# A decoder layer on one core: batch 0's front as its own order on each engine, adapters staged elsewhere

## The reference

```python
# attention, 16 heads of 32
q, k, v = heads(x @ Wq + bq), heads(x @ Wk + bk), heads(x @ Wv + bv)
scores = normalised(q) @ normalised(k).T / (sigmoid(x.mean(axis=1) @ Wt + bt) + 0.5)
vals, idx = top_k(scores, S // 4)            # keep the 64 largest of each row of 256
attn = softmax(vals) scattered to idx
gate = sigmoid(x @ Wg + bg)
x = layernorm(x + gate * ((attn @ v) @ Wo + bo) + (1 - gate) * x)
# cross attention with the context as key and value
s = (x @ xWq + xbq) @ (ctx @ xWk + xbk).T
x = layernorm(x + softmax(s) @ (ctx @ xWv + xbv))
# adapters: 8 of 32 matrices of 512 by 512, chosen by ids, summed with weights
x = layernorm(x + x @ sum_k(w[k] * W[ids[k]]).T + sum_k(w[k] * b[ids[k]]))
```

## Time and profile before

| | us |
|---|---|
| median of 3 runs (3546.75 to 3565.47) | 3558.0 |
| the profiled execution | 3552.69 |
| its span | 3550.8 |
| PE busy | 2939.5 (83%) |
| DVE busy | 2754.0 (78%) |
| ACT busy | 2140.6 (60%) |
| POOL busy | 1797.6 (51%) |

### The profile page before, as it was taken

One profiled execution on the slowest core, in us unless ns is written; L12 is line 12 of the kernel. 1 busy time (PEld: TensorE's weight loads), 2 busy tenths in 40 slices (PEclk: granted clock), 3 DMA queues, 4 the chain that ended last, 5 costly groups with the idle time before them and its releaser, 6 DMA issues. The chain is left out here.

```text
span 3550.8 us, 59586 instructions
## 1 busy us (share of the span) xinstructions
PE 2939.5 (83%) x16154; PEld 1615.6 (45%) x16154; DVE 2754.0 (78%) x9472; ACT 2140.6 (60%) x5970; POOL 1797.6 (51%) x2285
## 2 busy tenths in 40 slices
PE   6798988878898689797887889788988889879755
PEld 3344444444454345454444445444544444444433
DVE  3787877878787787887878778787878888778872
ACT  2666666656666456665655667566665666566541
POOL 4355545545544455454554455465544556446533
PEclk9899999989998899999999999999989999899977
DMA  5000000000000000000000000000000000000000
GB/s 204 7 16 22 22 23 19 23 4 23 22 22 19 4 22 22 22 20 4 23 22 22 20 22 5 22 23 22 22 20 5 23 22 23 22 19 16 4 16 12
DMA packets 43575, 80.46 MB, mean 23 GB/s; under 512 B 3786, under 2 KB 11978, under 8 KB 43058
## 3 DMA queue, kind: packets, MB, share of 16 engines
q1 hardware_dynamic: 41554, 69.18, 5.8%
q0 software_dynamic: 1504, 5.77, 0.5%
HBM read 58.16 MB, written 16.78 MB: 21 GB/s over the span
## 5 line engine op out<-in xcount | busy, mean ns | idle before, releaser
L517 POOL TENSOR_SCALAR probs<-probs,kept_inv 128x256 f32<-128x256 f32 x1024 | 528.7, 536 | 892.1 <-DVE kept_inv L1769 892.1
L1730 DVE SCALAR_TENSOR_TENSOR probs<-scores,threshold,probs 128x256 f32<-128x256 f32 x1006 | 432.4, 493 | 206.9 <-issue 134.7
L1029 PE MATMUL work_ps<-ident,probs 128*128 128x128 f32 x2072 | 333.0, 297 | 182.9 <-POOL probs L517 123.6
L807 ACT ACTIVATE probsT<-work_ps 128x512 f32<-128x512 f32 x512 | 294.4, 596 | 303.8 <-PE work_ps L1029 287.9
L772 ACT ACTIVATE scores<-score_ps,neg_guess 128x256 f32<-128x256 f32 x1024 | 397.1, 483 | 103.7 <-DVE kept_inv L1769 98.1
L792 ACT ACTIVATE near<-scores 128x256 f32<-128x256 f32 x1024 | 412.8, 421 | 24.3 <-DVE nearest L1698 22.5
L1694 DVE MATCH_REPLACE8 near<-nearest,near 128x256 f32<-128x256 f32 x1024 | 406.9, 407 | 0.0
L1690 DVE MAX8 nearest<-near 128x8 f32<-128x256 f32 x1024 | 358.3, 411 | 6.3 <-DVE near L1682 4.7
L1029 PEld LDWEIGHTS work_ps<-ident,probs 128*128 128x128 f32 x2072 | 241.6, 149 | 263.2 <-POOL probs L517 120.2
L1698 DVE MAX8 nearest<-near 128x8 f32<-128x256 f32 x1024 | 356.9, 409 | 0.0
L484 POOL TENSOR_TENSOR inv_norm<-sumsq,minus_half 128x32 f32<-128x32 f32 x64 | 351.3, 5490 | 5.3
(11 more groups left out here) (171 smaller groups left out, 5535.4 us busy)
## 6 DMA issues: line engine op xcount, KB each, us to landing
x_in<-in_x_dram SPq DMA_DIRECT2D x32, 512.0 KB, 3.9
x_res<-in_x_dram SPq DMA_DIRECT2D x32, 512.0 KB, 4.6
out_dram<-rows SPq DMA_DIRECT2D x32, 512.0 KB, 3.1
c_sb<-in_ctx_dram SPq DMA_DIRECT2D x32, 256.0 KB, 2.7
scores<-in_L_ffn_W_dram SPq DMA_DIRECT2D x6, 1024.0 KB, 6.8
near<-in_L_ffn_W_dram SPq DMA_DIRECT2D x2, 1024.0 KB, 10.0
w_q<-in_L_attn_Wq_dram POOLq DMA_DIRECT2D x1, 1024.0 KB, 8.1
w_k<-in_L_attn_Wk_dram POOLq DMA_DIRECT2D x1, 1024.0 KB, 10.0
```

The lines of the kernel that those rows point to most:

```text
L517: pool.tensor_scalar(probs[:, s % 2, h, j], probs[:, s % 2, h, j], kept_inv[:, s % 2, n:n + 1], 1.0, ALU.mult, ALU.mult).then_inc(s_pr, 1)
L807: act.activation(probsT[:, h, 2 * a:2 * a + 2], W[BANK_TP[s][2 * h + a]][:].rearrange("p (h k n) -> p h k n", h=2, k=NT), ACT.Copy).then_i ...
L1029: last = pe.transpose(dst[:, n * P:n * P + P], part, ident[:])
L1730: step.mark(dve.scalar_tensor_tensor(out=probs[:, r, h, j], in0=scores[:, r, h, j], scalar=threshold[:, r, k:k + 1], in1=probs[:, r, h, j] ...
```

## The change

The front of batch 0 is no longer written by the passes "fill" and "first" (each step in them has got a condition `where != "fill"` or `where != "first"`), but as a list of its own ahead of `body(-1, ...)` on each engine. `fuse()` is gone; its parts are steps of these lists. PE's list in full, since the others answer to it:

```diff
             setup()
+            turn_x(0, 0)
+            turn_x(0, 1)
+            key(0, 0)
+            pe.wait_ge(s_xt, 2)
+            temp(0)
+            query(0, 0)
+            pe.wait_ge(s_qc, 1)
+            query(0, 1)
+            pe.wait_ge(s_tmp, 1)
+            key(0, 1)
+            pe.wait_ge(s_xt, 1)
+            turn_raw(1, 0).then_inc(s_fill, 1)
...
+            turn_raw_key(6, 1).then_inc(s_fill, 1)
+            pe.wait_ge(s_empty, 3)
+            cross_weights(7, 0).then_inc(s_fill, 1)
+            pe.wait_ge(s_empty, 6)
+            turn_query(0, 0)
+            pe.wait_ge(s_empty, 4)
+            turn_key(0, 0)
...
+            cross_weights(9, 2).then_inc(s_fill, 1)
+            pe.wait_ge(s_q16, 1)
+            pe.wait_ge(s_qt, 1)
+            adapter_bias(10).then_inc(s_fill, 1)
+            pe.wait_ge(s_kt, 1)
+            turn_query(0, 1)
+            pe.wait_ge(s_empty, 10)
+            turn_key(0, 1)
...
+            key_sums(0)
+            pe.wait_ge(s_empty, 9)
+            key_moments(0)
+            pe.wait_ge(s_empty, 8)
+            cross_weights(11, 3).then_inc(s_fill, 1)
+            pe.wait_ge(s_kt, 2)
+            cross_bias(12).then_inc(s_fill, 1)
+            pe.wait_ge(s_m, 1)
+            row_means(0)
+            pe.wait_ge(s_mu, 1)
+            row_moments(0, 0)
+            pe.wait_ge(s_empty, 12)
+            row_moments(0, 1)
+            make_scores(0, 0, 0)
+            pe.wait_ge(s_qu, 1)
+            gate(0, 0)
+            pe.wait_ge(s_empty, 11)
+            gate(0, 1)
+            pe.wait_ge(s_kf, 1)
+            turn_adapters(13, 0).then_inc(s_fill, 1)
...
+            turn_adapters(16, 3).then_inc(s_fill, 1)
+            late_weights()
             body(-1, 1, "fill")
             body(0, 0, "first")
```

The parts of `fuse()` may now use all four banks (`FILL_BANK`), one bank per step. The adapters are staged in buffers that batch 1 uses first, in two halves each, and DVE adds them by halves:

```diff
-        f_stage = [scores[:, 0].rearrange("p a h k -> p (a h k)"), scores[:, 1].rearrange("p a h k -> p (a h k)"),
-                   near[:].rearrange("p a h k -> p (a h k)")]
+        f_stage = [[rows[:, 4], rows[:, 5]],
+                   [gate_t[:, 1].rearrange("p t d -> p (t d)"), v_sb[:, 1].rearrange("p t d -> p (t d)")],
+                   [kT[:, 1].rearrange("p g k -> p (g k)"), rows[:, 6]]]
```

The loads on SP are issued in another order. The ids come first, wt_cols and neg_bt have a semaphore of their own (`s_temp`), bq_cols is the last of the short vectors, the raw weights stand ahead of the id loads, and x of batch 1 stands ahead of adapter 5:

```diff
+                    sp.dma_start(ids_sb[:], fids.rearrange("(a k) -> a k", a=1)).then_inc(s_ids, 16)
+                    load_x(0)
+                    for b, (g, a) in ((abk, BK), (abq, BQ), (abg, BG), (abv, BV)):
...
+                    sp.dma_start(bq_cols[:], xbq.rearrange("(a p) -> p a", p=P)).then_inc(s_late, 16)
+                sp.wait_ge(s_wk, 16)
+                sp.dma_start(raw_wq, xWq.rearrange("(a p) n -> p a n", p=P)).then_inc(s_rawx, 16)
+                sp.dma_start(raw_wk, xWk.rearrange("(a p) n -> p a n", p=P)).then_inc(s_rawx, 16)
                 sp.wait_ge(s_ids, 16)
...
                 for k, n in enumerate(ids):
                     if k >= 3:
-                        sp.wait_ge(s_fused, k - 2)
+                        sp.wait_ge(s_fused, 2 * (k - 2))
+                    if k == 5:
+                        load_x(1)
```

DVE waits in `setup()` only for the four biases, and widens wt_cols after the split. ACT waits for neg_bt after it has taken the first key. In a product of batch 0 only the last matmul waits for the split biases:

```diff
-            def project(dst, src, w, bias, t, kts=KD):
+            def project(dst, src, w, bias, t, kts=KD, first=False):
                 for kt in range(kts):
                     pe.matmul(dst, src[:, kt, t * P:t * P + P], w[:, kt], start=kt == 0, stop=False)
+                if first:
+                    pe.wait_ge(s_bias, 1)
                 return add_bias(dst, bias)
```

DVE's list, in full:

```diff
             setup()
+            split_biases(0)
+            widen_temp()
+            key_sums(0, 0)
+            temperature(0)
+            query_sums(0, 0)
+            query_sums(0, 1)
+            adapters(0, 1)
+            key_sums(0, 1)
+            adapters(1, 2)
+            adapter_shares()
+            adapters(2, 3)
+            split_late_biases()
+            adapters(3, 4)
+            query_moments(0, 0)
+            query_moments(0, 1)
+            moments(0)
+            after_guesses()
+            adapters(4, 5)
+            adapters(5, 6)
+            adapters(6, 7)
+            adapters(7, 8)
```

More of the change, by code:

```diff
@@ L421, in _ @@
             load_ctx(0)
-            load_x(1)
             load_x(2)
@@ L570, in body @@
                 if ahead:
-                    norms(i + 1, 0)
+                    if where != "fill":
+                        norms(i + 1, 0)
                 if behind:
@@ L581, in body @@
                 if ahead:
-                    norms(i + 1, 1)
+                    if where != "fill":
+                        norms(i + 1, 1)
                 if behind:
@@ L593, in body @@
                 if ahead:
-                    guesses(i + 1)
+                    if where != "fill":
+                        guesses(i + 1)
                 if here:
@@ L603, in _ @@
             setup()
+            norms(0, 0)
+            normalise(0, 0)
+            norms(0, 1)
+            normalise(0, 1)
+            guesses(0)
             body(-1, 1, "fill")
@@ L909, in body @@
                 if here:
-                    if where == "first":
-                        fuse()
-                    exps(i, 0, 0)
+                    if where != "first":
+                        exps(i, 0, 0)
                 if behind:
@@ L915, in body @@
                 if here:
-                    exps(i, 0, 1)
+                    if where != "first":
+                        exps(i, 0, 1)
                 if behind:
@@ new lines, in turn_raw, with turn_raw_key, cross_weights @@
+            def turn_raw(n, et):
+                if n == 1:
+                    pe.wait_ge(s_rawx, 32)
+                return turn(W[FILL_BANK[n]], [raw_wq[:, dt, et * P:et * P + P] for dt in range(KD)])
+            def turn_raw_key(n, e2):
+                return turn(W[FILL_BANK[n]], [raw_wk[:, ct, et * P:et * P + P] for et in (2 * e2, 2 * e2 + 1)
+                                              for ct in range(KC)])
+            def cross_weights(n, dt):
+                pe.wait_ge(s_empty, TURNED)
+                for et in range(KD):
+                    mm = pe.matmul(W[FILL_BANK[n]][:, 0:C], wqT[:, et, dt * P:dt * P + P], wkT[:, et],
+                                   start=et == 0, stop=et == KD - 1)
+                return mm
@@ L1093, in fuse @@
-                pe.wait_ge(s_fused, NW)
-                pe.wait_ge(s_empty, n)
-                for dt in range(KD):
-                    n += 1
-                    if dt >= 2:
-                        pe.wait_ge(s_empty, n - 2)
-                    turn(T[n % 2], [f_sum[:, ot * D + dt * P:ot * D + dt * P + P] for ot in range(KD)])\
-                        .then_inc(s_fill, 1)
-                pe.wait_ge(s_empty, n)
+                return pe.matmul(W[FILL_BANK[n]][g * GROUP:g * GROUP + GROUP, :], f_w_cols[:], f_b_rows,
+                                 start=True, stop=True)
@@ L1102, in fuse, with turn_adapters, late_weights @@
+            def turn_adapters(n, dt):
+                if dt == 0:
+                    pe.wait_ge(s_fused, 2 * NW)
+                return turn(W[FILL_BANK[n]], [f_sum[:, ot * D + dt * P:ot * D + dt * P + P] for ot in range(KD)])
+            def late_weights():
                 pe.wait_ge(s_bias, 2)
@@ L1647, in key_sums @@
                    .then_inc(s_ssk, 1)
-                if isinstance(b, int) and b == 0 and t == 1:
-                    adapters(0, 3)
             def query_moments(b, t):
```

516 lines of the change are left out of this document (281 added, 235 removed).

## The result

| | before | after |
|---|---|---|
| median | 3557.7 us (3546.4 to 3566.5, 14 runs) | 3578.0 us (3568.1 to 3585.7, 14 runs) |
| profiled execution | 3552.7 us | 3576.6 us |
| its span | 3550.8 us | 3574.8 us |
| DVE busy | 2754.0 us | 2747.9 us |
| PE busy | 2939.5 us | 2949.3 us |

The ratio is 1.0062, with a 95% interval of 1.0050 to 1.0073: 20 us more, where 17 less (3540, range 3527 to 3556) were forecast.

The account below looks back on a forecast made before the run. The prediction took the waits in the start before the batch loop as the bound, neither PE nor DVE being full; the mark moving from 111.1 to 93.8 gave 17.3 us, 3558.0 less 17.3 rounded to 3540, range 3527 to 3556.

Parts of the forecast that it names:

- Small loads, products: Start of the front: DVE waits for fewer small loads, so the key product starts at 12.4, not 21.4: 9.0 us gained.
- POOL's norms: Second norms of batch 0: fewer adapter sums beside POOL, 1.1 us taken back (range 0 to 2.9), normalised at 45.2.
- rival 1: Front's load queues bite: late adapter 0 and load 7 expose waits of 4.5 us together; gain 11, 3547; chance 0.20.
- Adapters: Adapters 4 to 7, queued behind the guesses on DVE: adapter 7 ends at 70.5 us in place of 83.98.
- The new order's cost: Two value products now stand between last adapter and second scores: 14.0 us where 12.2 stood before, scores at 84.5.
- The reading of the Trainium skill that was set aside: Throttled clock is the default, so the first value product behind PE's idle gap is 1.5 us slower; gain 15.8.
- ACT: Stretch from second scores to the sides of quarter 1: 9.3 us, from 14.9 before less first signs and waits.
- The mark: DVE's sides of quarter 1, at 111.10 us before, forecast at 93.8; the end moves with it, less what slack swallows.
- Rival 2: Slack after the mark swallows half: up to 9 us lost if later waits grow; gain 8, 3550; chance 0.12.
- At nothing: Items priced at no cost: retained order after the front, batch 1's loads ahead of adapter 5, staging in batch 1's buffers.
- Rival 3: All slower: loop entered at another moment meets other clocks; 1.0 us a pass for 30 passes gives 3571; chance 0.08.
- The argument against it: Against the all-slower rival in the loop: a pass is ordered by its own waits, and no entry should be remembered.

Follow-up runs that it names:

- e2: Changed kernel with 8 instructions taken out of a never-run branch, so its loop code stands about where the kernel before has it: 3541.1 us, ratio 0.9954.
- e1: Kernel before with 8 jumped-over instructions added ahead of the VectorE loop, moving its code as the change does: 3593.8 us, ratio 1.0117.
- shifts 8 and 136: Loop code 8 or 136 instructions later than in the kernel before: the changed kernel itself, 3578.0 us, and with 128 more unexecuted instructions, 3587.0 us.
- e8: Changed kernel with its loop code moved by 136 instructions against the kernel before, 128 more than the change's own 8: 3587.0 us.
- e11: Kernel before with the two sides of keep_top's branch exchanged, so the common case is fallen into: 3535.6 us, ratio 0.9944.
- e13: Changed kernel with keep_top's common case first and 24 unexecuted instructions added in batch 0's first rare path: 3505.7 us, ratio 0.9864.
- e5: Changed kernel with 24 unexecuted instructions added, its loop code 32 later than in the kernel before: 3591.3 us.
- shifts 0 and 128: Changed kernel with loop code placed as in the kernel before (8 instructions removed), 3541.1 us, or 128 later (120 unexecuted added), 3542.7 us.
- e10: Changed kernel with the two sides of keep_top's branch exchanged, so the common case is fallen into: 3517.3 us, ratio 0.9890.
- shift 32: Changed kernel with loop code 32 instructions later than in the kernel before, by 24 unexecuted instructions: 3591.3 us.

## Why the prediction was wrong

Its sum for the front is not what made it wrong. Point by point:

- *Small loads, products.* The last bias landed at 11.0, not 9.1. The key product started at 13.3 (12.4 forecast), since w_k came 0.9 later, and took 6.41 in place of 5.80; so the second norms started at 36.5 (35.0).
- *POOL's norms* took 10.1 from clamp to scaled rows (36.46 to 46.54; 10.2 forecast), with a clamp of 1.15 and a power of 6.29. Neither adapter 0 nor neg_bt cost anything; rival 1 is out.
- *Adapters.* The guesses held adapter 4 back until 61.3 (60.0), the wait for the last load was 0.24 (about 1 forecast), and adapter 7 ended at 71.3 (70.5).
- *The new order's cost* is the term that was mis-sized: the second scores ended 15.7 behind the adapters, not 14.0. The first value product with its bias took 6.0 (76.07 to 82.06), not 4.4. The granted clock explains it:

```profile
71.00:75.00 4.00, 3.57 (x16) 3.27 (x16) 3.97 (x10) 1.79 (x3) 0.00 (x0) 0.50 0.03 10
75.00:82.00 7.00, 6.00 (x10) 2.32 (x9) 7.00 (x29) 0.60 (x1) 0.00 (x0) 0.63 0.00 0
```

  These are windows after (start, end, length, busy us and count of PE, PEld, DVE, ACT, POOL, then the granted clock): 0.50, which is 1.2 GHz, behind PE's idle 4.88 us, and 0.63 over the product. The reading of the Trainium skill that was set aside (the first value as slow as the one at 59.51, gain 15.8) was the better one.
- *ACT* took 9.3 behind the scores (86.94 to 96.24), as forecast.
- The mark moved by 14.9 (17.3 forecast, 14 to 20 called likely), and e2's median says that 15 to 16 us of it reach the end. Rival 2 is out.

The step that failed is the first of the *At nothing* list, "the retained order of everything after the front". The order was retained; its place in VectorE's program was not, and that place costs 37.5 us in the old front (e1) and 36.9 in the new one (changed kernel against e2), where the forecast had nothing. I counted the halved adapter sums as work (nothing, since the halves add up) and not as instructions, and the profile before showed 134.7 us of "issue" ahead of `probs` that I never asked about. Rival 3 had the sign and nearly the size (it priced 1.0 us a pass at 3571), which is luck, but not the cause: its mechanism, an entry that is remembered, is refuted by e1 and e2, and the mean granted clock is 0.930 before and 0.929 after. The argument against it, that a pass is ordered by its own waits, holds for semaphores and not for a wait that no semaphore shows.

What stays open: why a wait in which code is fetched is 1.5 us longer at one place and 3.2 at another, why place 8 waits 0.9 longer at shifts 8 and 136 with no packet in the wait, and the 9 us between e8 and the changed kernel.

## What to carry to other kernels

In a loop with taken jumps, look at the waits behind a jump that the profile calls "issue", and at the instruction packets in them: here they were a cost of code placement, and 8 instructions more, earlier in that engine's program, changed the time by 37 us. Before a small change to such a kernel is judged, pad the code with instructions that are jumped over, in both kernels, until both loops stand alike; the change's own worth is the difference there, to some 9 us as e8 shows. Put the common case where it is fallen into, so that the jump stands behind queued work: here that is worth 21 us (e11 against before) to 86 us (e13 against e5) and leaves 12 us of scatter between placements.

## What the hardware did that I had not expected

- Instruction waits repeat with a period of 128 instructions of the built program (shifts 0 and 128, 8 and 136). The Trainium skill (Runtime: NRT & Kernel Launch, "Instruction fetch mechanics") says that a taken branch whose target lies outside the window of two pages forces a fetch before execution can go on. The mechanism agrees with the packets seen inside the long waits; the blocks of 256 instructions that it gives do not agree with the period seen here nor with the packets of 8192 bytes, and the measurement decides.
- A wait behind a jump in which code is fetched is 1.5 to 3.2 us longer than the one at the same place without a fetch (1.21 to 2.73 at place 5, 1.21 to 3.46 at place 1, 1.13 to 4.28 at place 8).
- The first instruction of a trip waits for issue too, in every kernel and on two engines, which I take for the loop's own return: 29.4 us on DVE in 13 trips (before, `sumsq` for issue; 30.1 in e10), 41.6 us on PE in 13. On DVE a packet of 8192 bytes starts 1.9 us before the end of 11 of the 13. Nothing I tried changed it except shift 32 (16.9 on DVE); whether it can be hidden like the other was not tried.
- POOL's scaling of eight score rows takes 5.67 us beside DVE's turning and 3.68 when DVE waits, so that an instruction wait on DVE is paid again on POOL and PE.
